# Summing gathered fp32 rows as three bfloat16 parts instead of one fp32 product

## The reference, cut to what matters

```python
xl = x @ W.T + b                      # linear, so it is applied after the sum
msgs = xl[src]
agg = jax.ops.segment_sum(msgs, dst, num_segments=num_nodes)
cnt = jax.ops.segment_sum(jnp.ones((src.shape[0],), x.dtype), dst, num_segments=num_nodes)
return agg / jnp.maximum(cnt, 1.0)[:, None]
```

## Time and profile before

| | us |
|---|---|
| median of three runs | 7637.69 (7620.69 to 7654.07) |
| span of the profiled execution, first to last instruction | 7527.2 |
| median less that span | 110.5 |
| PE busy | 5373.7 (71%) |
| POOL busy | 4732.4 (63%) |
| DVE busy | 3160.7 (42%) |
| mean granted TensorE clock | 0.750 |

### The profile page before, as it was taken

One profiled execution on the slowest core, in us unless ns is written; L12 is line 12 of the kernel. 1 busy time (PEld: TensorE's weight loads), 2 busy tenths in 40 slices (PEclk: granted clock), 3 DMA queues, 4 the chain that ended last, 5 costly groups with the idle time before them and its releaser, 6 DMA issues. The chain is left out here.

```text
span 7527.2 us, 81611 instructions
## 1 busy us (share of the span) xinstructions
PE 5373.7 (71%) x17807; PEld 3065.0 (41%) x17807; DVE 3160.7 (42%) x6956; ACT 545.2 (7%) x1542; POOL 4732.4 (63%) x4778
## 2 busy tenths in 40 slices
PE   5666777638765556636566687788888888888887
PEld 2333333525332223324444575433433344444444
DVE  2222444528655556674444567511111123333317
ACT  0000000324000000010000001100000000000004
POOL 5666665664666666677677404766666666666665
PEclk8777777969767777767778899865555588888869
DMA  4444433331688888846667675433333333333445
GB/s 137 133 134 130 124 123 121 128 100 66 214 256 256 265 262 268 266 134 210 210 217 226 205 191 148 126 89 89 90 89 87 89 111 119 119 119 119 123 101 191
DMA packets 693161, 1164.20 MB, mean 155 GB/s; under 512 B 104128, under 2 KB 490285, under 8 KB 692614
## 3 DMA queue, kind: packets, MB, share of 16 engines
q0 software_dynamic: 224288, 633.55, 28.9%
q1 hardware_dynamic: 468344, 525.21, 21.9%
q10 hardware_dynamic: 110, 0.23, 0.0%
HBM read 870.83 MB, written 287.77 MB: 154 GB/s over the span
## 5 line engine op out<-in xcount | busy, mean ns | idle before, releaser
L2126 PE MATMUL l_sums<-big 128*128 (+1 forms) x3520 | 1701.9, 578 | 349.1 <-issue 135.1
L195 DVE TENSOR_TENSOR big<-iota_row,dst_tab 128x512 f32<-128x512 f32 x660 | 458.4, 695 | 2171.3 <-PE l_sums L2126 712.1
L1280 POOL DMA_INDIRECT bin_rows<-staging,place_tab x832 | 979.6, 1177 | 337.4 <-issue 249.1
L1166 POOL DMA_INDIRECT big<-kv_rows,idx_tab x880 | 832.0, 945 | 503.0 <-issue 241.1
L578 POOL DMA_INDIRECT big<-in_x,big x832 | 826.6, 994 | 483.6 <-SPq L148 237.7
L2083 POOL DMA_INDIRECT big<-x_rows,place_tab x880 | 882.3, 1003 | 394.9 <-issue 241.7
L2083 POOL DMA_INDIRECT big<-x_rows,idx_tab x832 | 817.2, 982 | 426.7 <-issue 226.6
L1220 PE MATMUL es_q<-big 128*128 x1760 | 720.9, 536 | 450.3 <-issue 343.3
L2126 PEld LDWEIGHTS l_sums<-big 128*128 128x128 f32 x3520 | 765.2, 259 | 502.0 <-issue 473.7
L612 PE MATMUL l_sums<-big 128*128 x1760 | 723.0, 543 | 331.9 <-issue 235.8
L1504 PE MATMUL ws_sums<-big 128*128 128x264 f32 x1760 | 546.1, 474 | 321.2 <-DVE big L1524 170.9
(11 more groups left out here) (297 smaller groups left out, 5187.4 us busy)
## 6 DMA issues: line engine op xcount, KB each, us to landing
v_edge<-big SPq DMA_DIRECT2D x880, 128.0 KB
big<-v_edge SPq DMA_DIRECT2D x220, 512.0 KB
bin_rows<-big SPq DMA_DIRECT2D x110, 520.0 KB
sims<-bin_rows SPq DMA_DIRECT2D x110, 520.0 KB
staging<-in_edges SPq DMA_DIRECT2D x104, 520.0 KB
gate_rows<-big SPq DMA_DIRECT2D x49, 512.0 KB
big<-gate_rows SPq DMA_DIRECT2D x49, 512.0 KB
big<-kv_rows,idx_tab POOLq DMA_INDIRECT x880
```

What stands on the lines that cost most here:

```text
L195: return dve.tensor_tensor(out, rows, columns.unsqueeze(2).to_broadcast([P, QUAD, P]), ALU.is_equal)
L1166: pool.indirect_dma_start(ring[:, u, :], None, k.kv_rows, bass.IndirectOffsetOnAxis(ap=k.idx[:, s:s + 1], axis=0)).then_inc(s_row[u], 16)
L1280: pool.indirect_dma_start(k.bin_rows, bass.IndirectOffsetOnAxis(ap=k.place[:, c:c + 1], axis=0), k.staging[:, g % 2, j, :], None).then_inc ...
L2126: pe.matmul(sums[:, bank_of(node[u] + turn, D)], onehot[:, u % HALF, :], flat[:, bass.ds(at, D)], start=False, stop=True, skip_group_check ...
```

## The change

The state is kept in DRAM a second time, as three bfloat16 parts: `high` is x rounded to bfloat16, `rest` is x less high in fp32, `middle` is rest rounded, `low` is rest less middle. The parts are made in `attend_close` by two ACT copies and two DVE subtractions per window and sent by one more DMA of 192 KB per window into `x3_parts` (1,536 B per node). Both turns of `last_gathers` gather those rows, the one-hots are written as bfloat16, each fp32 product becomes three bfloat16 products into the same bank, and `push` is gone. The fp32 rows are still written, for the layer's end.

```diff
-def push(pe, k, spare):
-
-    ones = k.ones.bitcast(BF16)
-    pe.matmul(spare, ones[:, 0:1], ones[:, 0:1], start=True, stop=True)
...
+            def send_parts(w, slot, nodes):
+                sp.wait_ge(s_low, w + 1)
+                sp.dma_start(k.x3_parts[bass.ds(w * P, P), :], parts[:, slot, :]).then_inc(s_parts[slot], 16)
+
-            over(sp, (load, 0), (send, 6))
+            over(sp, (load, 0), (send, 6), (send_parts, 8))
...
+            def high_part(w, slot, nodes):
+
+                act.wait_ge(s_new, w + 1)
+                if not early(w, S):
+                    act.wait_ge(s_parts[slot], turns(w, slot, 1))
+                act.copy(parts[:, slot, 0:D], x[:, node_window(w)]).then_inc(s_high, 1)
+
+            def middle_part(w, slot, nodes):
+
+                act.wait_ge(s_rest, w + 1)
+                act.copy(parts[:, slot, D:2 * D], rest[:, slot, :]).then_inc(s_middle, 1)
+
-            over(act, (second_root, 3), (first_root, 2), (copy_turned, 0))
+            over(act, (second_root, 3), (first_root, 2), (copy_turned, 0), (high_part, 5), (middle_part, 6))
...
+            def take_high(w, slot, nodes):
+
+                dve.wait_ge(s_high, w + 1)
+                dve.tensor_tensor(rest[:, slot, :], x[:, node_window(w)], parts[:, slot, 0:D],
+                                  ALU.subtract).then_inc(s_rest, 1)
+
+            def low_part(w, slot, nodes):
+
+                dve.wait_ge(s_middle, w + 1)
+                dve.tensor_tensor(parts[:, slot, 2 * D:], rest[:, slot, :], parts[:, slot, D:2 * D],
+                                  ALU.subtract).then_inc(s_low, 1)
...
-                 (second_moments, 3))
+                 (second_moments, 3), (take_high, 6), (low_part, 7))
...
-        ring = room.take([P, U, D])
+        ring = room.take([P, U, PARTS * D], BF16)
         flat = ring.rearrange("p u d -> p (u d)")
-        onehot = room.take([P, HALF, P])
+        onehot = room.take([P, HALF, P], BF16)
...
-                pool.indirect_dma_start(ring[:, u, :], None, k.x3_rows, bass.IndirectOffsetOnAxis(
+                pool.indirect_dma_start(ring[:, u, :], None, k.x3_parts, bass.IndirectOffsetOnAxis(
...
-                at = u * D if turn else slot_of(t, node[u], D)
+                at = u * PARTS * D if turn else slot_of(t, node[u], PARTS * D)
...
-                pe.matmul(sums[:, bank_of(node[u] + turn, D)], onehot[:, u % HALF, :], flat[:, bass.ds(at, D)],
-                          start=False, stop=True, skip_group_check=True).then_inc(s_sum, 1)
-                push(pe, k, spare[:, 0:1])
+                for n in range(PARTS):
+                    ins = pe.matmul(sums[:, bank_of(node[u] + turn, D)], onehot[:, u % HALF, :], flat[:, bass.ds(at + n * D, D)],
+                                    start=False, stop=True, skip_group_check=True)
+                ins.then_inc(s_sum, 1)
```

More of the change, by code:

```diff
@@ L55 @@
 DEGMAX = 511
+PARTS = 3
 assert (NW - 1 - 4) % 4 == 0
@@ L1634, in attend_close @@
         part = sets.take([P, S, D])
+        parts = sets.take([P, S, PARTS * D], BF16)
+        rest = room.take([P, S, D])
         tps = [psum(nc, ctx, f"ac_t{i}", [P, 512]) for i in range(2)]
@@ L1647, in attend_close @@
         s_gate = sems(nc, k, *(f"nt_gate{i}" for i in range(S)))
+        s_high, s_rest, s_middle, s_low = sems(nc, k, *(f"sp_{n}" for n in ("high", "rest", "middle", "low")))
+        s_parts = sems(nc, k, *(f"sp_sent{i}" for i in range(S)))
         block = ctx.enter_context(nc.Block())
@@ L1669, in send @@
                 sp.dma_start(k.x3_rows[bass.ds(w * P, P), :], x[:, node_window(w)]).then_inc(s_sent, 16)
-            over(sp, (load, 0), (send, 6))
+            def send_parts(w, slot, nodes):
+                sp.wait_ge(s_low, w + 1)
+                sp.dma_start(k.x3_parts[bass.ds(w * P, P), :], parts[:, slot, :]).then_inc(s_parts[slot], 16)
+            over(sp, (load, 0), (send, 6), (send_parts, 8))
             sp.wait_ge(s_sent, 16 * NW)
+            for slot in range(S):
+                sp.wait_ge(s_parts[slot], 16 * len(range(slot, NW, S)))
         @block.gpsimd
@@ L2060, in last_gathers @@
         sums = psum(nc, ctx, "l3_sums", [P, BANKS * BANK])
-        spare = psum(nc, ctx, "l3_spare", [1, BANK])
         s_zeros, s_hot, s_sum, s_taken, s_free, s_lasts, s_here, s_used = sems(nc, k, *(f"l3_{n}" for n in (
@@ L2339, in build @@
         k.x3_rows = dram("x3_rows", [NPAD, D]).ap()
+        k.x3_parts = dram("x3_parts", [NPAD, PARTS * D], BF16).ap()
         k.node_gates = dram("node_gates", [NPAD, D]).ap()
```

## The result

The changed kernel takes 7795.53 us (median of 4 runs, 7774.67 to 7815.29); the kernel before, run beside it, 7632.96 (4 runs, 7620.69 to 7654.07). The ratio is 1.0216, with a 95% interval from 1.0186 to 1.0247: 2.2% slower, 163 us. The prediction was 7565 us with a range up to 7710; the time lies outside it, on the other side of no change.

What follows compares the result with a forecast made beforehand. DVE was taken to bound attend_close, PE and POOL together turn 1, PE turn 2. Terms of +42, -30, -80 and -6 sum to -74 us: span 7453.2 plus 110.5 around it, called 7565 us, range 7410 to 7710.

Steps and rivals of the forecast that it cites:

- +42 for attend_close: attend_close: two more subtractions per window on a DVE with no room, plus 2 us at the end; range +35 to +79.
- -30 for turn 1: Turn 1 of last_gathers: a sixth of the possible gain from shorter PE array work, -30 us, range -165 to +60.
- -80 - 6 for turn 2: Turn 2 of last_gathers: iterations fall to 21.4 us, -80 us, range -105 to +60; the last 96 steps save 6.
- the price of the address instructions: Turn 1: two more address instructions per step, 90 ns at the median but up to 1401 in PE's slow spells.
- the reading that PE's work is the bound: Turn 2: PE, not POOL, sets the 23.0 us iteration, by some 2 us over POOL's 20.9.
- the stretches at the half clock: Turn 2: the 3.5 us per iteration left over after PE's work and one wait, put down to the slow clock.
- the rival that had 0.22: The gathers don't move, as waits between engines set the pace; only attend_close counts, 7680 to 7698 us; chance 0.22.
- The upper bound of 61: Turn 1: the 164 us above PE's dense pitch, grown with instructions per step from 8 to 11, 61 us.
- The one-hots, the gathers and the products: last_gathers: bfloat16 one-hots and 1.5 KB gathers cost 0; three products take 0.45 us at full clock, 0.90 at half.
- Rival 3: Turn 2 falls to the half clock throughout, +206 us in place of -80, total 7856 us; chance 0.06.
- 110.5 us lie around the span: Whole kernel: 110.5 us added to the predicted span of 7453.2 us to give the timed 7563.7.

Runs made afterwards that it cites:

- e17: The changed kernel with one of its three products, the high parts alone, in both turns, on the slower chip: 1.0097 to the kernel before.
- e12: The changed kernel with one of its three products, the high parts alone, in both turns, on a faster chip: 1.0041 to the kernel before.
- e0: The kernel before, unedited, run for a second trace; it fell on a faster chip: 6647 us, one run.
- e15: The changed kernel once more, unedited, on a faster chip: 1.0076 to the kernel before.
- e7: The changed kernel with 16 one-hots in place of 8, made 12 steps ahead and not 4, on the slower chip: 1.0222 to the kernel before.
- e16: The kernel before with PE loading 32 blocks at a time into registers in place of 16, on the slower chip: 0.9988.
- e5: The changed kernel with turn 1's three products reading fixed zeros, without register addresses, on the slower chip: 1.0004 to the kernel before, 7634 us.
- e6: The kernel before with three spare one-column products per step of turn 1, columns picked by register, in place of one, on the slower chip: 1.0104.
- e1: The kernel before plus the parts made and sent in attend_close, which nobody reads, on a faster chip: 1.0042, 28 us.
- e4: The changed kernel once more, unedited, on the slower chip: 1.02 to the kernel before, 7779 us.
- e3: The kernel before without its spare one-column product, on a faster chip: 0.9998.
- e9: The kernel before with PE loading 32 blocks at a time into registers in place of 16, on a faster chip: 0.9991.
- e13: The kernel before with PE loading 32 blocks at a time into registers in place of 16, repeated on a faster chip: 0.9998.

## Why the prediction was wrong

The forecast was +42 for attend_close, -30 for turn 1 and -80 - 6 for turn 2, together -74 us. The traces have +21, +150 and +8. So the largest miss is turn 1, by 180 us, and the second is turn 2, by 94. Two steps failed: in turn 1 the size and the upper bound of the price of the address instructions, and in turn 2 the reading that PE's work is the bound.

**Turn 2: the reading of the bound failed, and with it the largest term of the sum.** The step was: "So PE is the bound of turn 2, by some 2 us per iteration over POOL", from which -80 us came. It rests on 3.5 us that were left over and put down to "the stretches at the half clock"; that remainder was never read from a row. The rows at hand allowed another sum: POOL's own 20.9 us and the 2.3 us in which it stands still are 23.2, about the whole iteration of 23.0. e17 takes two thirds of the array work away and the iteration stays at 16 x 1.443 = 23.1 us; on B the same kernel (e12) takes 16 x 1.291 = 20.7. For turn 2 on A the rival that had 0.22 is right, "the waits between PE, SP and POOL set the pace and not the array"; its total of 7680 to 7698 us was too low by a hundred, as it gave turn 1 no loss.

What the wait looks like in the changed kernel's turn 2 (from the timeline of all engines; start, duration, idle before and releaser):

```profile
6761.35 0.82 PE L2155 MATMUL l_sums<-big 128*128 128x256 bf16 x6
6761.36 0.95 POOL L2111 DMA_INDIRECT big<-x_parts,place_tab  x1 [0.30 <-issue]
...
6763.39 0.75 DVE L2011 SCALAR_TENSOR_TENSOR big<-sims,big 128x512 f32<-128x512 f32 x1
...
6767.77 0.94 POOL L2111 DMA_INDIRECT big<-x_parts,place_tab  x1 [0.30 <-issue]
6770.54 0.69 DVE L190 TENSOR_TENSOR big<-iota_row,bin_tab 128x512 bf16<-128x512 f32 x1 [6.40 <-remote]
6770.71 1.35 POOL L2111 DMA_INDIRECT big<-x_parts,place_tab  x1 [2.00 <-remote]
...
6771.72 1.67 PE L2155 MATMUL l_sums<-big 128*128 128x256 bf16 x7 [9.56 <-DVE big L190]
```

PE's last products end at 6762.2 by the trace. VectorE, which waits for the semaphore that they raise, is let go at 6770.5, 8 us later, and POOL within 0.2 us of it. PE stands idle 9.56 us, and such waits take up whatever its array saves. In most iterations of 16 steps POOL is held up at one place: 66 of its 879 distances from gather to gather are over 1.8 us in the changed kernel, 58 in the kernel before, none on B (e0, e15). The cause of the lateness stays open. Runs speak against the array (e17), the lead of the one-hots (e7) and the register load (e16). The spare product is no cause either, since of the two kernels of the result the one has it and the other not, at 1.452 and 1.461 us. Nor does the loading of PE's program fit: the instruction queue whose count follows the length of that program (q8 of the profile) moved 37 pieces in the 49 iterations of the changed kernel and 24 in those of e17, which take as long. On B POOL has the pace and the wait costs nothing.

**Turn 1: the mechanism was named, but its size and the sign of the term were wrong.** The term was -30 us, "a sixth of the possible gain", range up to +60. It measured +150 in the traces, and e5 gives 144 back by taking out the register addresses. The upper bound of 61 was three eighths of the 164 us above PE's dense pitch, for three more instructions on eight. That supposed that slow instructions grow in number with the program and that each costs the same whatever else PE does. The traces contradict it. The register instructions of PE between the first and the last gather of turn 1, on A, counted in the traces:

| | per step | in all | over 0.3 us | turn 1, us |
|---|---|---|---|---|
| kernel before | 6 | 5231 | 380 | 1232.7 |
| changed kernel | 8 | 6940 | 379 | 1382.3 |
| e5, fixed rows | 5 | 4364 | 533 | 1229.4 |
| e6, three spare products | 9 | 7809 | 249 | 1326.3 |
| e17, one product | 6 | 5211 | 494 | 1288.8 |

There are as many slow instructions in the changed kernel as before, and most in the quickest; e6 has more register instructions than the changed kernel and is 56 us faster. So neither count gives the price (time lost between two instructions is in neither). What remains is how much of a stall comes through to the loop. In the fp32 kernel a step's array work is 1.24 us long, and a stall of 0.7 us in the sequencer is partly hidden behind products that are still queued. With 0.82 us of products of which each needs its own address first, less is hidden. That account agrees with e17 (an array even shorter, 1288.8 us against 1232.7 with the same count of register instructions) and with e6 (an array even longer), but it is argued and not shown: e17 also gathers 1.5 KB rows and has no spare product, and the changed kernel with its spare product back was not run on A. The larger rows are not a cost by themselves, as e5 has them too and takes 1229.4.

**attend_close: the mechanism was right and the size, on most runs, too large.** The term was +42 with a range from +35 (its parts, 41 and 2, are 43); the windows differ by 21 us, and e1 measures 28 on B. The stage is not steady on A: from its first gather to the first of turn 1 it takes 203.0 to 208.3 us without the parts (e16, the kernel before, e6), and with them 216.8 and 218.0 (e5, e4), 229.2 (the result) and 243.0 (e17). The subtractions of the changed kernel, and an older one that the earlier trace rows has at a median of 782 ns in the kernel before:

```profile
L1868 DVE TENSOR_TENSOR sims<-xs,big x49: 385/390/1349, 4726.5 to 4924.9; 128x256 f32<-128x256 f32 x49
```

```profile
L1874 DVE TENSOR_TENSOR big<-sims,big x49: 410/851/945, 4731.0 to 4925.8; 128x256 bf16<-128x256 f32 x49
```

```profile
L1807 DVE TENSOR_TENSOR big<-big,sims x49: 398/402/1473, 4702.4 to 4910.2; 128x256 f32<-128x256 f32 x49
```

One new subtraction takes 390 ns and the other 851, near the 0.42 and 0.79 that the bounds had. But the older one fell from 782 to 402. The trace shows what goes with it: the instances of the two under 0.6 us share at most 2% of their time with an elementwise operation of POOL, and the longer ones 70%. The first subtraction doesn't follow this, with 390 ns at 62% of overlap. The overlap is not the change's doing alone, since the older instruction takes 401 ns in the kernel before on B (e0). A stage's DVE time is then not the old sum plus the new instructions; here two were added and the busy time grew by 218 - 199 = 19 us, one cheap subtraction's worth.

**The one-hots, the gathers and the products** took what was forecast. POOL takes 946 ns for a gather of 1.5 KB as for one of 1 KB, VectorE 689 ns for the comparison, PE 0.82 us for three products at the half clock (by the timeline, where the last end is modelled) where 0.9 was taken. The last 96 steps take 134 us where 135 stood; the 6 us of the forecast did not come. Rival 3, a clock under 0.7 in turn 2, did not come (0.77). By the Trainium skill, TensorE: Matmul & The Clock Gate, section Why this matters for your kernels, idle gaps between bursts of matmuls bring the slow clock back; the trace agrees, with 0.51 in turn 1 and 0.77 in turn 2 where 0.57 and 0.86 stood. Idle time alone doesn't tell it, since e5's turn 1 was granted 0.64 with PE idle for more than half of it. Since the array did not pace turn 2 on A, the slower clock cost nothing there; for turn 1 no run shows it.

**The base.** That 110.5 us lie around the span was wrong as well: a timed run is 2 us longer than its span (7815.29 and 7813.6 in the profiled one), and the other 108 us were the distance of a quick execution from the median. The forecast is the median less 74 either way.

Could a version beat both? The runs point to none. The kernel with parts pays 28 us in attend_close (e1) and more in turn 1, for array time that turn 2 doesn't wait for, and the edits to the kernel before that keep its result (e3, e9, e13, e16) are within 0.15% of it.

## What to carry to other kernels

Before taking array time out of a loop, explain the pace of the loop to the last tenth of a us. A remainder that is put down to "the clock" or "some stalls" is where the bound may lie, and the test is cheap: a run with the product cut to a third shows at once whether the array is waited for. Count the sequencer instructions of a split as well as its columns: three products with register addresses are three address computations, and the max beside the median (1395 beside 36 ns) tells that such instructions have a tail on this chip. But don't multiply the tail by the count: in turn 1 two more of them per step came with no more slow ones and 150 us. A busy share that falls while the pace stays, with the idle time under another name after each edit (one-hots, then issue), points to a wait further back that no engine's own work explains.

## What the runs showed of the hardware

- Three chips ran one and the same program in 6654 to 6665 us, and a fourth in 7519 and 7634. A gather takes POOL 946 ns at the median on both; what differs is the waits between the engines.
- On the slower one, register instructions of PE that take 36 ns at the median take up to 1.4 us, in bursts, in first_gather and turn 1. In turn 2 hardly any do (4 over 0.3 us in the kernel before, 6 and 18 in two traces of the changed one), but 149 with one product (e17).
- On it, VectorE and POOL were let go together 8 us after PE's last products in turn 2, and POOL is held up so, for shorter or longer, about once per 16 steps.
- One and the same VectorE subtraction of a stage took 782 ns at the median in the kernel before on A, 402 in the changed kernel there, and 401 in the kernel before on B; the long instances lie beside POOL's elementwise work.
